# Experts' stage of a two-layer kernel: order of maxima and result scaling, queue of the weights, a small stage folded in

## The reference, cut to what matters

```python
# attention of layer 1, the factor that mixes its two halves
l1 = jnp.exp(jnp.minimum((lambda_q1 * lambda_k1).sum((-1, -2)), 5.0))
l2 = jnp.exp(jnp.minimum((lambda_q2 * lambda_k2).sum((-1, -2)), 5.0))
lv = (l1 - l2 + LAMBDA_INIT).mean()
a1 = jax.nn.softmax(jnp.einsum('bhnd,bhmd->bhnm', q1, k1) * scale, axis=-1)
...
out = jnp.concatenate([x1 - lv * x2, x2], axis=-1) @ Wp.T + bp
```

## Time and profile before

| | |
|---|---|
| median of 3 runs | 5118.35 us (5115.52 to 5127.24) |
| profiled execution, its own time | 5121.19 us |
| its span | 5119.4 us |
| PE busy in the span | 4428.4 us (87%) |
| DVE busy | 4293.8 us (84%) |
| ACT busy | 3667.3 us (72%) |
| POOL busy | 1507.7 us (29%) |
| mean granted PE clock | 0.957 of full |
| stage of the experts with `mix_factor` | about 1682 to 2535 us |

### The profile page before, as it was taken

The page is one execution under the profiler, slowest core; times in us unless marked ns, Lnnn a source line. Parts: engine busy times, 40 slices in busy tenths (PEclk is TensorE's granted clock), DMA queues, the critical chain, the costliest instruction groups (busy, mean ns, idle before and its releaser), DMA issues. The chain is left out here.

```text
span 5119.4 us, 91604 instructions
## 1 busy us (share of the span) xinstructions
PE 4428.4 (87%) x33121; PEld 1766.3 (35%) x33129; DVE 4293.8 (84%) x5014; ACT 3667.3 (72%) x6263; POOL 1507.7 (29%) x1024
## 2 busy tenths in 40 slices
PE   5768778777776588899899998999998999999998
PEld 3225225225223354555422222222222222222225
DVE  5997997898897454545499999999998999999996
ACT  5765765666663233333399998899998999999993
POOL 1883983883884100000011111021111311121003
PEclk8998998998998798999999999999999999999999
DMA  2402102101202212122111112121112211212016
GB/s 84 152 0 100 33 1 74 58 1 47 69 1 86 85 59 75 59 70 70 52 35 39 36 35 46 37 53 35 37 38 50 52 37 37 52 50 71 22 28 186
DMA packets 302468, 275.39 MB, mean 54 GB/s; under 512 B 167923, under 2 KB 264014, under 8 KB 299406
## 3 DMA queue, kind: packets, MB, share of 16 engines
q1 hardware_dynamic: 264590, 155.79, 11.2%
q0 software_dynamic: 33136, 111.58, 7.1%
q10 hardware_dynamic: 4352, 2.66, 0.2%
HBM read 150.17 MB, written 118.69 MB: 53 GB/s over the span
## 5 line engine op out<-in xcount | busy, mean ns | idle before, releaser
L1776 DVE TENSOR_REDUCE at_mpart<-at_ps 128x1 f32<-128x1024 f32 x2048 | 2348.6, 1211 | 95.5 <-PE at_ps L1665 60.0
L1761 ACT ACTIVATE at_E<-at_ps 128x512 f32<-128x512 f32 x4096 | 2221.3, 595 | 169.7 <-PE at_ps L1680 85.0
L1687 PE MATMUL at_ps<-at_E,at_vst 128*32 128x256 f32 x16400 | 1315.7, 392 | 23.0 <-ACT at_osb L1742 18.6
L1665 PE MATMUL at_ps<-at_ks,at_qs 48*128 48x512 f16 x4096 | 802.3, 388 | 59.4 <-DVE at_mpart L1776 27.9
L1680 PE MATMUL at_ps<-at_qs,at_ks 50*128 50x512 f16 x4096 | 792.0, 383 | 21.0 <-ACT at_E L1761 19.9
L887 POOL TENSOR_TENSOR l_work<-l_work 128x1024 f32<-128x1024 f32 x256 | 604.6, 2362 | 78.5 <-DVE l_work L896 70.1
L1549 POOL DMA_INDIRECT at_y<-yd,at_gidx x128 | 129.4, 1011 | 1677.8 <-DVE at_mx L1781 1592.3
L783 PE MATMUL l_ps<-l_bc,l_sel 96*128 96x512 bf16 x1024 | 313.4, 395 | 268.6 <-DVE l_work L896 126.7
L1687 PEld LDWEIGHTS at_ps<-at_E,at_vst 128*32 128x32 f32 x16400 | 326.4, 108 | 564.1 <-issue 410.1
L1665 PEld LDWEIGHTS at_ps<-at_ks,at_qs 48*128 48x128 f16 x4096 | 196.5, 93 | 880.1 <-DVE at_mpart L1776 455.1
L821 PE MATMUL l_ps<-l_work,l_ident 128*128 128x512 f32 x1024 | 482.2, 592 | 5.1 <-DVE l_work L917 5.1
(11 more groups left out here) (268 smaller groups left out, 4143.2 us busy)
## 6 DMA issues: line engine op xcount, KB each, us to landing
xd<-l_zero SPq DMA_DIRECT2D x4, 5120.0 KB, 33.0
yd<-at_late POOLq DMA_DIRECT2D x40, 512.0 KB, 3.0
at_late<-xd POOLq DMA_DIRECT2D x38, 512.0 KB, 4.8
at_qs<-qp SPq DMA_DIRECT2D x132, 128.0 KB
at_ks<-kp SPq DMA_DIRECT2D x396, 32.0 KB
at_late<-in_eW POOLq DMA_DIRECT2D x7, 1536.0 KB, 8.0
ot<-at_osb SPq DMA_DIRECT2D x516, 17.0 KB
at_qs<-qp SPq DMA_DIRECT2D x132, 64.0 KB
```

Of the source, the lines that this page charges most:

```text
L1665: mm = pe.matmul(ring[n % 2][:, r, :], m.qs[row, buf, bass.ts(i, P)], m.ks[row, buf, bass.ts(kh, BANK)], start=True, stop=True)
L1687: mm = pe.matmul(O[32 * q:32 * q + 32, :], m.vst[:, par, SLOTS_A * kk + sl, :], m.E[:, sl % 4, kk, bass.ts(q, QG)], start=(sl == 0 and kk ...
L1761: act.activation(m.E[:, sl % 4, kk, bass.ts(hf, BANK)], S[chunk(sl, 2 * hf + kk) % 3], ACT.Exp, scale=scale).then_inc(s.ex, 1)
L1776: dve.tensor_reduce(m.mpart[:, job:job + 1], ring[n % 2].rearrange("p a b -> p (a b)"), AX_X, ALU.max).then_inc(s.ring_free, 1)
```

## The change

- `mix_factor` is gone as a stage. Its loads are issued inside `run_experts`: lambdas and late weights by ACT, rows, identity and first weights by SP in another order. Its DVE and ACT instructions stand at the head of the streams of `run_experts`; the first rows are turned before the norms of the first weights.
- `mix_sums`, `mix_mean` and `bias_parts` hold the instructions of lines 1134 to 1149 and 1490 to 1498 unchanged; `first_peak` and `first_low_row` are `first_peaks` cut in two.
- The two first maxima of a block stand inside it on both engines: one behind hidden 0 (PE) and product 0 (DVE), one before hidden 3 (PE) and behind rows_low(n+1, 1) (DVE). The wait for "limits" stands before hidden 0 of the block.
- `results(n-1)` stands at the end of block n on DVE, behind the last hidden_low. rows_low(n+1, 1) stands where it was.
- The weights of experts 1 to 7 are issued by SP, each after the split of the expert before it, among SP's loads of the first heads. POOL's stream is otherwise the same.
- The buffer fills are POOL memsets at the start of its stream, one after another. The turn of the maxima is used by ACT and DVE one block earlier.

```diff
@@ -1103,51 +1103,7 @@
 
 def load_weights(eng, io, m, e):
 
-    eng.dma_start(m.wst, io.eW[bass.ts(e, P), :]).then_inc(io.wg0 if e else io.w_first, 16)
-
-
-def mix_factor(nc, io, m):
...
-            def _(sp):
-                load_weights(sp, io, m, 0)
-                for n, v in enumerate((io.lambda_q1, io.lambda_k1, io.lambda_q2, io.lambda_k2)):
-                    sp.dma_start(m.lam[:, n, :], v.rearrange("a b c -> (a b c)").partition_broadcast(P)).then_inc(s.w_in, 16)
-                for t, v in ((m.ident, io.ident), (m.wp, io.WpT.rearrange("(c p) n -> p c n", p=P)), (m.brow, io.bp.partition_broadcast(1))):
-                    sp.dma_start(t, v).then_inc(s.w_in, 16)
-                for n in range(2):
-                    load_rows(sp, io, m, n)
-                sp.wait_ge(s.w_in, 16 * 7)
...
+    eng.dma_start(m.wst, io.eW[bass.ts(e, P), :]).then_inc(io.wg0, 16)
...
-def first_loads(sp, io, m, a):
-
-    load, load_v, rows = attention_loads(sp, io, m, a)
-    sp.wait_ge(a.init, 5)
-    load(0, 0)
-    sp.wait_ge(a.loaded, LOAD)
-    load(1, 1)
-    load_v(0, 0)
-    rows(0, 0, 0)
-    sp.wait_ge(a.loaded, 2 * LOAD)
-    sp.wait_ge(a.v_loaded, 16)
-    sp.wait_ge(a.mrow, 64)
...
-        PEAK_AT, TURN_AT, LOW_AT = 4, 12, 13
+        PEAK_AT, TURN_AT, LOW_AT = 4, 12, 12
...
-            return range(2 * (n - PEAK_AT), 2 * (n - PEAK_AT) + 2) if PEAK_AT <= n < AFTER_ALL else ()
+            return 2 * (n - PEAK_AT) if PEAK_AT <= n < AFTER_ALL else None
...
@@ -1227,10 +1169,33 @@
 
             @block.sync
             def _(sp):
+                load, load_v, rows = attention_loads(sp, io, m, a)
+
+                def next_weights(e):
+                    sp.wait_ge(s.wlo, 2 * e)
+                    load_weights(sp, io, m, e)
+
+                load_rows(sp, io, m, 0)
+                sp.dma_start(m.ident, io.ident).then_inc(s.ident_in, 16)
+                load_weights(sp, io, m, 0)
+                load_rows(sp, io, m, 1)
+                next_weights(1)
                 sp.wait_ge(s.split, 5)
                 for r in range(2):
                     sp.dma_start(m.bp3[:, r, :], m.bpart).then_inc(s.spread, 16)
-                first_loads(sp, io, m, a)
+                sp.wait_ge(a.init, 5)
+                load(0, 0)
+                sp.wait_ge(a.loaded, LOAD)
+                load(1, 1)
+                load_v(0, 0)
+                next_weights(2)
+                next_weights(3)
+                rows(0, 0, 0)
+                for e in range(4, E1):
+                    next_weights(e)
+                sp.wait_ge(a.loaded, 2 * LOAD)
+                sp.wait_ge(a.v_loaded, 16)
+                sp.wait_ge(a.mrow, 64)
                 sp.wait_ge(s.spread, 32)
...
+                pool.memset(m.E[:, 3, :, :], 1.0).then_inc(a.init, 1)
+                pool.wait_ge(a.init, 1)
+                pool.memset(m.vst, 0.0).then_inc(a.init, 1)
+                pool.wait_ge(a.init, 2)
+                pool.memset(m.vst[:, :, :, HD:HD + 1], 1.0).then_inc(a.init, 1)
+                pool.wait_ge(a.init, 3)
+                pool.memset(m.ks[32:64, :, :], 2.0 ** ROW_EXP).then_inc(a.init, 1)
+                pool.wait_ge(a.init, 4)
+                pool.memset(m.ks[96:128, :, :], 2.0 ** ROW_EXP).then_inc(a.init, 1)
+                pool.wait_ge(a.init, 5)
                 for n in range(BLOCKS):
-                    e = n // PER + 1
-                    if n % PER == 0 and e < E1:
-                        pool.wait_ge(s.wlo, 2 * e)
-                        load_weights(pool, io, m, e)
                     if 1 <= n < BLOCKS - 1:
                         pool.wait_ge(s.turned, KD * n)
                         load_rows(pool, io, m, n + 1)
@@ -1258,6 +1229,8 @@
                 def norms(e, n):
 
                     pe.wait_ge(s.squares, e + 1)
+                    if e == 0:
+                        pe.wait_ge(s.ones, 1)
                     if peaks_before(n):
                         pe.wait_ge(a.ring_free, peaks_before(n))
                     if e:
@@ -1322,15 +1295,21 @@
...
-                norms(0, 0)
+                pe.wait_ge(s.ident_in, 16)
                 for k in range(KD):
                     turn(0, k)
+                norms(0, 0)
                 for n in range(BLOCKS):
                     e = n // PER
                     if n % PER == 0:
                         pe.wait_ge(s.wlo, 2 * (e + 1))
                     pe.wait_ge(s.xlo, KD * (n + 1))
+                    first = peaks(n)
+                    if first is not None:
+                        pe.wait_ge(s.limits, (n - PREPARE + PER - 1) // PER + 1)
                     hidden(n, 0)
+                    if first is not None:
+                        peak(first)
                     hidden(n, 1)
                     if n + 1 < BLOCKS:
                         turn(n + 1, 0)
@@ -1339,11 +1318,9 @@
                     hidden(n, 2)
                     if n + 1 < BLOCKS:
                         turn(n + 1, 1)
+                    if first is not None:
+                        peak(first + 1)
                     hidden(n, 3)
-                    for job in peaks(n):
-                        if job % 2 == 0:
-                            pe.wait_ge(s.limits, (n - PREPARE + PER - 1) // PER + 1)
-                        peak(job)
                     if n == TURN_AT - 1:
...
+                for n, v in enumerate((io.lambda_q1, io.lambda_k1, io.lambda_q2, io.lambda_k2)):
+                    act.dma_start(m.lam[:, n, :], v.rearrange("a b c -> (a b c)").partition_broadcast(P)).then_inc(s.lam_in, 16)
+                for t, v in ((m.wp, io.WpT.rearrange("(c p) n -> p c n", p=P)), (m.brow, io.bp.partition_broadcast(1))):
+                    act.dma_start(t, v).then_inc(s.late_in, 16)
+                rows_high(0, 0)
+                act.wait_ge(s.lam_low, 1)
+                act.activation(m.lsum[:, 4:6, :], m.lsum[:, 2:4, :], ACT.Exp).then_inc(s.lam_ex, 1)
+                rows_high(0, 1)
                 squares(0)
                 weights_high(0)
-                for k in range(KD):
-                    rows_high(0, k)
...
-                    if n == TURN_AT:
+                    if n == TURN_AT - 1:
...
+                dve.memset(m.one3, 1.0)
+                dve.memset(m.ones, 1.0).then_inc(s.ones, 1)
+                mix_sums()
+                rows_low(0, 0)
+                rows_low(0, 1)
+                mix_mean()
                 scales(0)
                 weights_low(0)
-                for k in range(KD):
-                    rows_low(0, k)
-                dve.memset(m.one3, 1.0)
-                dve.tensor_copy(m.bpart[:, 0, :], m.brow).then_inc(s.split, 1)
-                dve.wait_ge(s.split, 1)
-                dve.tensor_tensor(m.brest[:, 0, :], m.brow, m.bpart[:, 0, :], ALU.subtract).then_inc(s.split, 1)
-                dve.wait_ge(s.split, 2)
-                dve.tensor_copy(m.bpart[:, 1, :], m.brest[:, 0, :]).then_inc(s.split, 1)
-                dve.wait_ge(s.split, 3)
-                dve.tensor_tensor(m.brest[:, 1, :], m.brest[:, 0, :], m.bpart[:, 1, :], ALU.subtract).then_inc(s.split, 1)
-                dve.wait_ge(s.split, 4)
-                dve.tensor_copy(m.bpart[:, 2, :], m.brest[:, 1, :]).then_inc(s.split, 1)
-                dve.memset(m.E[:, 3, :, :], 1.0).then_inc(a.init, 1)
-                dve.memset(m.vst, 0.0).then_inc(a.init, 1)
-                dve.wait_ge(a.init, 2)
-                dve.memset(m.vst[:, :, :, HD:HD + 1], 1.0).then_inc(a.init, 1)
-                dve.memset(m.ks[32:64, :, :], 2.0 ** ROW_EXP).then_inc(a.init, 1)
-                dve.memset(m.ks[96:128, :, :], 2.0 ** ROW_EXP).then_inc(a.init, 1)
+                bias_parts()
...
                 for n in range(BLOCKS):
+                    first = peaks(n)
                     for mt in range(MT):
                         product(n, mt)
                         if mt:
                             hidden_low(n, mt - 1)
-                        if mt == 1 and n + 1 < BLOCKS:
-                            rows_low(n + 1, 0)
-                        if mt == 2:
-                            if n:
-                                results(n - 1)
-                            if n + 1 < BLOCKS:
-                                rows_low(n + 1, 1)
+                        if mt in (1, 2) and n + 1 < BLOCKS:
+                            rows_low(n + 1, mt - 1)
+                        if mt == 0 and first is not None:
+                            first_peak(first)
+                        if mt == 2 and first is not None:
+                            first_peak(first + 1)
                     hidden_low(n, MT - 1)
-                    first_peaks(n)
+                    if n:
+                        results(n - 1)
+                    first_low_row(n)
                     e = n // PER
...
             m = named(**t, **first)
-            mix_factor(nc, io, m)
             run_experts(nc, io, m, attention)
```

(36 more changed lines are left out.)

61 lines of the change are left out of this document (19 added, 42 removed).

## The result

The changed kernel takes 5170.11 us (median of 4 runs, 5167.64 to 5179.69) against 5121.0 of the kernel before (4 runs): ratio 1.0099, 95% interval 1.008 to 1.0118. It is 49 us slower; the forecast was 5190, 73 more than the 5118.35 then known, with a range of 5135 to 5230. The profiled execution took 5167.70, 46.5 more than the one before, with a span of 5165.9.

The account below looks back on a forecast made before the run. DVE's order bounded blocks with maxima, PE the others, row loads nearly all. After: 37 x (20.7 + 1.5) + 7 + 4 = 832.4 against 742.95, 89 more; less 17, plus 1: +73, 5190 us, range 5135 to 5230.

Parts of the forecast that it names:

- The mechanism: Row loads in POOL's stream move with the scaling, 3.91 us later; PE waits 3.7 us at turn 0, blocks 2 to 38.
- The cycle: Serial path from turn 0 through scaling, store and row load to the next turn: 20.7 us a block instead of 16.9.
- The clock term: Output matmuls behind each row wait slow as PE's granted clock falls: 1.5 us a block, bounds nothing and 2.0.
- Limits: Wait for "limits" before hidden 0 of blocks 8, 13 and 18: some 3.4 us, mostly overlapping the row wait; 4 us added.
- Maxima in mid-block: The 3.0 us reduction wait goes, but row loads bound these 16 blocks; the second maximum adds 16 x 0.4 = 7 us.
- The head: Start of the stage, before the blocks: four gains summing to 17 us, bounds 12 to 21.
- Step (a): Start of the stage: squares start earlier, at the first weights' landing between 1690.5 and 1695; gain 2 to 6 us, 4 taken.
- Step (b): Start of the stage: first rows are turned while the weights are underway, so hidden 0 starts sooner; gain 3.2 us.
- step (c): Start of the stage: DVE's buffer fills no longer hold back the first product, for which PE waited; gain 7.2 us.
- Step (d): Start of the stage: PE's low clock after its wait for the first product is avoided; gain about 3 us.
- The fills: Buffer fills on POOL at the start: between 7.2 and 26 us, upper end taken, lying beside other work.
- The tail: End of the stage: the last outputs wait for the scaling before them, 1.3 us more.

## Why the prediction was right, and where it was off

**The mechanism was right.** The load's slack was the 0.2 us read in the earlier trace rows: the scaling moved, the distances 1.57 and 2.10 behind it stayed, and in 34 of the 37 cycles foreseen PE waited for the load, 3.1 us each; in the other three the wait for "limits" took its place. Putting back the scaling, or issuing the load an iteration earlier, takes every one of these waits away and 138 us of stage. The total is nearer than its parts, which is luck: of the some 24 us by which +73 overshoots +49, the cycles gave 28 and the tail 2 too much, and the head, forecast with 5 too much gain, took 5 back.

**The cycle**: 20.7 predicted. The cycles in which the clock did not fall are mostly 20.4 to 20.6 without maxima (2550.93 is 20.43 behind the scaling before it), 0.25 less. The load's issue to the turn took 4.68 there (2532.60 to 2537.28), where the working had 4.85 and 0.1. That is 37 x 0.25 = 9 us.

**The clock term was mis-sized.** "I take 1.5 a block" put a fall of the clock behind every wait. The loss by the groups of PE is 29.9/37 = 0.8 a cycle. It is the largest error: 26 us, of 28 by which 832.4 overshoots 804.3 (9 more came from the cycle, and 7 too few were taken for "limits"). The price of a fall was right, and the count was not: behind 16 of the 34 row waits the outputs took 6.3 to 7.9 us, together 24.6 over 5.40 or 1.5 each, and behind the other 18 they took 5.40. The length of the wait did not decide it. Two waits of the changed kernel:

```profile
2343.04 0.66 PE L1253 MATMUL at_ps<-at_ident,at_late 128*128 128x128 f32 x4 [2.70 <-DMA at_late<-xd]
2343.54 7.07 PE L1280 MATMUL at_ps<-at_wparts,at_late 128*128 128x256 f16 x48
...
2537.28 0.66 PE L1253 MATMUL at_ps<-at_ident,at_late 128*128 128x128 f32 x4 [3.74 <-DMA at_late<-xd]
2537.77 5.40 PE L1280 MATMUL at_ps<-at_wparts,at_late 128*128 128x256 f16 x48
```

Two waits of the earlier trace rows, both with a fall, were too few to tell how often one comes. The bounds 0 and 2.0 held the term; the 2.0 of the maxima blocks had other losses in it. What decides whether the clock falls behind a wait, these runs do not show.

**Limits**: 4 us were added for three waits of 3.4, and the waits are there, 10.2 in all. The overlap was right, and a term was missing: the clock fell behind these waits too.

```profile
1877.54 5.28 PE L1267 MATMUL at_ps<-at_late,at_wparts 128*128 128x512 f16 x12 [3.33 <-issue]
...
1989.69 4.22 PE L1267 MATMUL at_ps<-at_late,at_wparts 128*128 128x512 f16 x12 [3.52 <-issue]
...
2098.81 4.28 PE L1267 MATMUL at_ps<-at_late,at_wparts 128*128 128x512 f16 x12 [3.33 <-issue]
```

Elsewhere 12 such matmuls take 2.75, so 5.5 us were lost here. The three cycles take 24.9, 23.8 and 23.7 us, which is 9.7 over three cycles of 20.45 + 0.43 (the second maximum); less the 5.5 this leaves 1.4 a cycle, and 1.3 was taken. The sum of all cycles agrees: 804.3 - 37 x 20.45 - 6.9 - 29.9 = 10.9, which leaves about 1 us for the 13 waits for ACT (11.5 us, the experts' preparation). They lay beside the row waits.

**Maxima in mid-block** were said to be bound by the row wait. They are, at 353.6/16 = 22.1 us, against 20.7 + 1.5 + 0.4 = 22.6 by the working. The reduction's wait is gone and a row wait of like length has come, which is why only 11 us are gained over the earlier trace rows.

**The head** was too large by 5 us: 17 predicted, 11.7 measured (70.9 to 63.1, with the 3.9 of the new place). Step (a) failed. The timeline:

```profile
1695.54 0.49 DVE L1469 TENSOR_TENSOR at_late<-at_late 128x128 f32<-128x128 f32 x2 [11.85 <-DMA at_late<-in_lambda_k]
...
1697.40 1.11 PE L1253 MATMUL at_ps<-at_ident,at_late 128*128 128x128 f32 x4 [6.89 <-DVE at_late L1432]
...
1699.05 2.75 ACT L1335 ACTIVATE at_late<-at_late 128x3072 bf16<-128x3072 f32 x1
```

The weights landed 9.7 us after their issue at 1684.15, at 1693.9, inside the 1690.5 to 1695 of the working. But I had let "ACT's six issues and Exp lie before that landing". The lambdas landed last, at 1695.5; DVE waited for them with rows_low(0, 0) queued behind, PE's second turn waited for DVE, ACT for PE, and the squares stood behind. It is the very kind of wait that the prediction should have followed: a small DMA, and what is queued behind the engine that waits for it. Squares came 0.5 us later after the start than before, not 4 earlier. Step (b), 3.2, and step (c), 7.2, are there: the first hidden matmul is 2.7 earlier after the start (3.2 less that 0.5), and the wait for the first product is gone. Step (d), 3 us at the low clock, gave 1.8: from the first hidden matmul to the scaling of block 0 are 38.1 us before and 33.0 after, 9.0 less with the 3.9 of the new place, of which 7.2 is step (c). Together the four steps gave 11.7. The clock was low elsewhere instead: the first 24 hidden matmuls took 8.31 us, behind a wait of 9.0 for the split, where they had taken 7.02.

**The fills**: POOL was done in about 10.2 us (1683.30 to 1693.45), far below the upper bound of 26 taken from elementwise rows. It lay beside the rest, so it cost nothing.

**The tail**: 1.3 more predicted, 0.7 less measured (4.6 shorter, of which 3.9 is the place). Why was not looked into.

**The signs**: 34 waits for `xd` came instead of some 37, 3.1 us on average, 1.4 to 4.0; the scalings without maxima are 20.4 to 23.4 us apart; the reduction's wait is gone; the clock from 2200 to 2500 went from 0.99 to 0.94, not to 0.92; the first hidden matmul came 2.7 us earlier and not 7.

**The landing of the load.** By the Trainium skill, "DMA: Bandwidth & Descriptors" (Anatomy of one DMA), the estimate is that the load lands 3.9 us after its issue. With the store ahead of it the median was 4.7, and the cycle measured is the one with 4.7. By the same formula of the Trainium skill the estimate for one DMA of 512 KB is 3.2 us. The stores took 3.0, and the one row load with no store ahead of it (issued at 1699.12) took 3.7. So the estimate falls short by 0.5 us for a load alone and by 0.8 behind a store. The port lock of the Trainium skill's "SBUF — State Buffer" (two separate sides) can't be tested here: of DVE only two memsets of 0.17 us ran beside POOL's fills.

## What to carry to other kernels

Before moving an instruction, look at what waits for it on other engines' queues, and at what is queued behind that wait: here a prefetch that needed nothing from the scaling stood behind a store that did. Measure the slack of a prefetch (landing to use) before anything ahead of it moves; a slack of 0.2 us shows in no list of waits. And issue a prefetch as soon as its buffer is free, ahead of the waits in the same stream. Here one iteration earlier was enough: with that, neither the scaling's place nor the queue of the weights mattered, and the changed kernel went from 1% slower to 2% faster than the kernel before. Last, price a fall of the clock by how often it comes as well as by what one costs.

## What the runs showed of the hardware

- A POOL memset was as fast as DVE's: 3.50 us for 32x4096 of 16 bits, where DVE took 3.47, and 1.80 for 128x2048 of 32 bits, where DVE took 1.76. The elementwise rows of POOL were no guide. Both rows are of the changed kernel's head:

```profile
1683.30 1.80 POOL L1207 MEMSET at_E<- 128x2048 f32 x1 [5.08 <-POOLq L59]
...
1686.38 3.50 POOL L1213 MEMSET at_ks<- 32x4096 f16 x1
```

- Of 34 waits of PE of 1.4 to 4.0 us, one to a cycle of 20 to 23, 16 had slower matmuls behind them, at 1.5 us for 48 outputs, and 18 had none. A wait of 2.3 us had 7.07 us of outputs behind it, three of 3.7 to 3.8 had 5.40. Over all 37 cycles this is 0.8 a cycle. Two waits of 4.1 and 4.4 in the kernel before had cost 1.7 and 1.3.
- A load of 512 KB issued by POOL 0.53 us behind a store of 512 KB landed after 4.7 us (median); the one with no store ahead landed after 3.7.
- Four broadcast loads of the lambdas (64 KB each, written to 128 partitions) on ACT's queue took 5.2 to 10.9 us to land beside 2.6 MB of loads on SP's queue, and the last came in 1.6 us after the 1.5 MB of weights.
